# Four chunks of layer 1's attention values: from the context projection to the selective scan

## The reference

```
x = x + xattn0(layernorm(x), ctx, ctx)      # 16 heads of 32
x = x + scan(layernorm(x))                  # selective scan, 8 states, 256 inner channels
x = x + moe0(layernorm(x))
x = x + xattn1(layernorm(x), ctx, ctx)
x = x + delta_rule(layernorm(x))
x = x + moe1(layernorm(x))

def xattn(q, k, v):
    qp, kp, vp = q @ W_q + b_q, k @ W_k + b_k, v @ W_v + b_v
    out = softmax(qh @ kh.T / sqrt(32)) @ vh        # per head
    return out_of_heads @ W_o + b_o
```

## Time and profile before

| | us |
|---|---|
| median of 3 runs | 3893.53 |
| lowest, highest | 3889.25, 3896.72 |
| the profiled execution | 3890.58 |
| its span, first to last instruction | 3889.3 |
| projection, to attention's first matmul | 0 to 815.9 |
| attention of layer 0, to its last exchange | 815.9 to 1720 |
| scan stage | 1720 to 1825 |
| experts of layer 0, queries of layer 1 | 1825 to about 2165 |
| mean granted TensorE clock, share of full speed | 0.957 |

### The profile page before, as it was taken

One profiled execution on the slowest core, in us unless ns is written; L12 is line 12 of the kernel. 1 busy time (PEld: TensorE's weight loads), 2 busy tenths in 40 slices (PEclk: granted clock), 3 DMA queues, 4 the chain that ended last, 5 costly groups with the idle time before them and its releaser, 6 DMA issues. The chain is left out here.

```text
span 3889.3 us, 46028 instructions
## 1 busy us (share of the span) xinstructions
PE 3610.6 (93%) x17868; PEld 2320.1 (60%) x17868; DVE 2531.3 (65%) x3462; ACT 1920.3 (49%) x1962; POOL 1775.6 (46%) x744
## 2 busy tenths in 40 slices
PE   7999999989999999986797999999999886799997
PEld 6777778755555555432674545555554475688886
DVE  3222234357777777637796877777776465699997
ACT  2112311245555555542683455555556321577775
POOL 1112111159999999920000599999998320100000
PEclk9999999999999999996897899999999998899999
DMA  7555565543333333102686233333331101799996
GB/s 274 181 180 178 189 197 173 176 133 91 86 87 77 85 87 87 38 23 109 272 358 211 55 83 91 85 87 79 85 87 30 49 1 44 289 372 369 377 379 251
DMA packets 215944, 593.83 MB, mean 153 GB/s; under 512 B 42624, under 2 KB 108192, under 8 KB 161840
## 3 DMA queue, kind: packets, MB, share of 16 engines
q1 hardware_dynamic: 176944, 517.47, 40.9%
q10 hardware_dynamic: 36864, 67.13, 4.6%
q0 software_dynamic: 1920, 6.29, 0.5%
HBM read 470.64 MB, written 120.09 MB: 152 GB/s over the span
## 5 line engine op out<-in xcount | busy, mean ns | idle before, releaser
L642 DVE TENSOR_REDUCE maxima<-psum 128x1 f32<-128x512 f32 x2048 | 1290.8, 683 | 387.3 <-PE psum L637 383.7
L751 ACT ACTIVATE pt<-psum 128x1024 f32<-128x1024 f32 x1024 | 1018.7, 1025 | 703.1 <-PE psum L662 697.6
L765 POOL TENSOR_TENSOR exp_sums<-pt 128x1024 f32<-128x1024 f32 x342 | 818.5, 2394 | 266.4 <-PE psum L678 132.4
L637 PE MATMUL psum<-ks,first_q 96*128 96x512 f32 x2048 | 815.0, 447 | 22.0 <-DMA first_q<-q_parts 9.2
L768 POOL TENSOR_TENSOR exp_sums<-exp_sums,pt 128x1024 f32<-128x1024 f32 x310 | 737.0, 2377 | 45.7 <-ACT pt L751 1.4
L637 PEld LDWEIGHTS psum<-ks,first_q 96*128 96x128 f32 x2048 | 394.3, 193 | 480.9 <-DVE maxima L642 326.0
L674 PE MATMUL psum<-pt,vs 128*32 128x512 f32 x4096 | 675.8, 600 | 4.7 <-DVE head_rows L778 2.3
L678 PE MATMUL psum<-exp_sums,constants 128*32 128x512 f32 x1408 | 671.7, 600 | 0.0
L662 PE MATMUL psum<-qs,ks 97*128 97x512 f32 x2048 | 648.7, 400 | 15.1 <-ACT pt L751 15.1
L1428 DVE TENSOR_TENSOR moe_cut<-moe_raw,moe_cut 128x2048 fp32r<-128x2048 f32 x244 | 557.1, 2291 | 55.6 <-ACT moe_cut L1370 50.9
L1370 ACT CAST moe_cut<-moe_raw 128x2048 fp32r<-128x2048 f32 x244 | 467.1, 1921 | 64.7 <-PE psum L97 64.7
(11 more groups left out here) (310 smaller groups left out, 4401.3 us busy)
## 6 DMA issues: line engine op xcount, KB each, us to landing
moe_raw<-in_moe_w SPq DMA_DIRECT2D x244, 1024.0 KB, 7.8
ks<-k_parts SPq DMA_DIRECT2D x384, 256.0 KB, 4.7
k_parts<-kparts ACTq DMA_DIRECT2D x256, 256.0 KB, 3.0
cx<-in_ctx SPq DMA_DIRECT2D x32, 1024.0 KB
v_heads<-vrow SPq DMA_DIRECT2D x32, 1024.0 KB, 5.8
vs<-v_heads SPq DMA_DIRECT2D x32, 1024.0 KB, 5.3
first_q<-q_parts SPq DMA_DIRECT2D x96, 64.0 KB, 4.1
qs<-q_parts SPq DMA_DIRECT2D x96, 64.0 KB, 4.8
```

What stands on the lines that cost most here:

```text
L637: pe.matmul(self.c.bank[self.FIRST_BANK + k % 3], self.first_q[s][:, t * P:(t + 1) * P], self.ks[s][part][0:3 * DH, at:at + CHUNK], start= ...
L642: dve.tensor_reduce(self.maxima[:, h % 2, i % TT, i // TT:i // TT + 1], self.c.bank[self.FIRST_BANK + k % 3], X, ALU.max).then_inc(*self.f ...
L751: act.activation(self.pt[:, self.slot(h, b) + i:self.slot(h, b) + i + 2, :], self.c.psum[:, at:at + 2, :], ACT.Exp).then_inc(*self.exp.up())
L765: engine.tensor_tensor(to, self.pt[:, slot:slot + R, :], self.pt[:, slot + R:slot + 2 * R, :], ALU.add).then_inc(*signal.up())
```

## The change

Late chunks are n = 9, 11, 13 and 15 of layer 1, which are m = 25, 27, 29 and 31. Of these the projection makes keys only. The context chunks are the same for both layers, so SP stores both parts of each late chunk's context from `cparts` to `late_context` already in layer 0, in chunks 9, 11, 13 and 15 (four stores of 512 KB per chunk, in rows of 512 bytes out of SBUF), and in chunk 17 both parts of layer 1's value weights to `late_weights` (2 MB). The cast two chunks later (11, 13, 15, 17) also waits for the stores of the parts. In the scan stage a new class `LateValues` loads the weights (2 MB) and the context (16 tiles of 512 KB, room for four) and makes 16 units of 12 matmuls in banks 0 and 1: three (`FIRST_LATE`) before the first add, then one after each add. ScalarE copies unit i out of PSUM right behind the decay of step i, and SP stores each chunk's values.

The values' bias isn't added in the projection any more: VectorE copies value blocks there. In attention it loads `bv` (256 KB, broadcast) and adds its columns to each head's finished rows, in both layers; the last transposes wait for that add. The constants lose `pick` (1024 columns, 512 KB, not read by anything). The norm of the scan gives its memory back early, and the context tiles take its place: SP loads the first of them once the scan's first product is made.

```diff
@@ ProjectContext @@
+    LATE = (9, 11, 13, 15)
-            self.bv = c.sb(st, "bv", [P, 2, D], side="right")
+        def store_parts(m):
+            if m in self.LATE:
+                late = self.LATE.index(m)
+                sp.wait_ge(*self.ctx_low.at(m + 1))
+                for t in range(CHUNK // P):
+                    sp.dma_start(S["late_context"][...], self.cparts[:, m % 2, :, :, t * P:(t + 1) * P]...)
...
+            if m == NCHUNK + 1:
+                sp.wait_ge(*self.w_low.at(4))
+                for part in range(2):
+                    sp.dma_start(S["late_weights"][part]..., self.w["v"][part][:]...)
...
@@ on_pe, on_act, on_dve @@
+            if m - NCHUNK in self.LATE:
+                continue
...
-                dve.tensor_tensor(self.vrow[:, :, t, :], bank..., self.bv[:, l, :]..., ALU.add)
+                dve.tensor_copy(self.vrow[:, :, t, :], bank...)
...
@@ split_chunk on ScalarE @@
+            if m - 2 in self.LATE:
+                act.wait_ge(*self.parts_out.at((self.LATE.index(m - 2) + 1) * (CHUNK // P)))
@@ CrossAttention.finish_head on VectorE @@
+            rows = self.rows[:, :, h * DH:(h + 1) * DH]
+            dve.tensor_tensor(rows, folded[:, :, 0:DH], self.total..., ALU.mult).then_inc(*self.finished.up())
+            if h == 0:
+                dve.wait_ge(*self.wo_in.at(3))
+            dve.wait_ge(*self.finished.at(h + 1))
+            dve.tensor_tensor(rows, rows, self.bv[:, None, h * DH:(h + 1) * DH].to_broadcast([P, TT, DH]), ALU.add).then_inc(*self.biased.up())
@@ CrossAttention.on_pe, before the last transposes @@
-        pe.wait_ge(*self.finished.at(HEADS))
+        pe.wait_ge(*self.biased.at(HEADS))
@@ LateValues @@
+    def load_context(self, sp, u):
+        if u >= self.ROOM:
+            sp.wait_ge(*self.made.at(u - self.ROOM + 1))
+        sp.dma_start(self.context[:, u % self.ROOM]..., self.S["late_context"][...])
+    def on_pe(self, pe, u):
+        pe.wait_ge(*self.context_in[u % self.ROOM].at(u // self.ROOM + 1))
+        if u > 1:
+            pe.wait_ge(*self.copied.at(u - 1))
+        for k in range(KD):
+            last = product(pe, self.banks[u % 2], [self.context[...]], [self.w[...]], k == 0, k == KD - 1)
+        last.then_inc(*self.made.up())
+    def on_act(self, act, u):
+        act.wait_ge(*self.made.at(u + 1))
+        act.copy(self.rows[:, i % 2, :, t, :], self.banks[u % 2]...).then_inc(*self.copied.up())
@@ SelectiveScan @@
+        self.late.load_weights(sp)
+        sp.wait_ge(*self.h_made.at(KD))
+        for u in range(self.late.ROOM):
+            self.late.load_context(sp, u)
...
+        for u in range(self.FIRST_LATE):
+            self.late.on_pe(pe, u)
         for i in range(self.STEPS):
-            if i:
-                add(i - 1)
-        add(self.STEPS - 1)
+            add(i)
+            if self.FIRST_LATE + i < self.late.units:
+                self.late.on_pe(pe, self.FIRST_LATE + i)
...
         for i in range(self.STEPS):
             decays(i)
+            if i < self.late.units:
+                self.late.on_act(act, i)
```

More of the change, by code:

```diff
@@ L230, in on_pe @@
                 last.then_inc(*self.k_made.up())
-                beside(m * self.UNITS + b)
+                beside(self.unit(m) + b)
+            if m - NCHUNK in self.LATE:
+                continue
             if n == 0:
@@ L240, in on_pe @@
                 last.then_inc(*self.v_made.up())
-                beside(m * self.UNITS + KD + t)
+                beside(self.unit(m) + KD + t)
     def on_act(self, act):
@@ L293, in on_act @@
                 split_chunk(m + 1)
-            for t in range(CHUNK // P):
-                beside(m * self.UNITS + KD + t)
+            for t in range(CHUNK // P if m - NCHUNK not in self.LATE else 0):
+                beside(self.unit(m) + KD + t)
     def on_dve(self, dve):
@@ L327, in on_dve @@
                     split_weights(3)
-                beside(m * self.UNITS + b)
+                beside(self.unit(m) + b)
+            if m - NCHUNK in self.LATE:
+                continue
             if m:
-                dve.wait_ge(*self.v_out.at(m))
+                dve.wait_ge(*self.v_out.at(self.valued(m)))
             for t in range(CHUNK // P):
@@ L817 @@
     CB, TAPS, RING = INNER // P, 3, 3
+    FIRST_LATE = 3
     STEPS = DSTATE * CB
@@ L854, in run @@
             self.y_made, self.out_made, self.x_added = c.signals(st, "y_made scan_out_made scan_x_added")
+            with ExitStack() as place:
+                self.norm = Normalize(c, place, self.x, "ln_s")
+            self.late.hold_context(st)
             self.loads(c.sp)
@@ L858, in run @@
             self.on_pe(c.pe)
+            for s in self.late.out:
+                c.sp.wait_ge(*s.all())
             c.barrier()
@@ L872, in loads @@
             sp.dma_start(self.terms[:, which], self.S["bc"][which].rearrange("s n -> (s n)").partition_broadcast(P).rearrange("p (s n) -> p s n", s=DSTATE)).then_inc(*self.term_in[which].up())
+        for u in range(self.late.ROOM, self.late.units + self.late.TILES):
+            if u < self.late.units:
+                self.late.load_context(sp, u)
+            if u % self.late.TILES == self.late.TILES - 1:
+                self.late.store(sp, u // self.late.TILES - 1)
     def on_pe(self, pe):
@@ L1980, in constants @@
         "spare": (EXPERTS + j[:, :TT]) * P + i,
-        "pick": np.concatenate([(i == s) & (j >= 0) for s in range(DSTATE)], 1),
     }
```

92 lines of the change are left out of this document (67 added, 25 removed).

## The result

The changed kernel took 3904.8 us (median of 11 runs, 3898.0 to 3912.5), the kernel before 3892.0 (11 runs, 3887.6 to 3896.7): ratio 1.0035, 95% interval 1.0025 to 1.0044. By the ratio that is 13.6 us slower (9.7 to 17.1), by more than the 0.2% that a measurement can tell. The forecast was +1.6, a change that can't be measured. The time lies in the stated range, but above the forecast's own band (3887 to 3903), in the case "slower" that had 0.28.

The account below looks back on a forecast made before the run. TensorE bounds attention and seemingly the projection, where a second chain through ScalarE and GpSimd is almost as long. The terms 0.3 - 12.2 + 2 + 4 - 0.8 + 5.8 + 2 + 0.5 gave +1.6 us: 3895 us, range 3882 to 3911.

Parts of the forecast that it names:

- case "slower": Whole kernel: slower by over 0.2%, made up of rivals 2 to 4 and the forecast's upper edge; chance 0.28.
- opening: Projection's start: value biases and constants not loaded, 1 MB less among the loads; -0.8 us (0 to -1.5).
- heads: Attention: each bias add waits behind GpSimd, first scores come late; +2 us (0 to +8), and +0.5 at layer ends.
- saved parts: Chunks 9, 11, 13, 15: context stores compete with key stores, 0.5 us each; +2 us (0 to +20).
- weights: Chunk 17: 2 MB in long rows delays key stores, TensorE lacks parts; +4 us (+1 to +6).
- scan: Scan stage: ScalarE's copy ahead of the decay lengthens steps, +4.7 us; second decay waits, +1.1; together +5.8 (+4.6 to +7).
- late chunks: Chunks 25 to 30: chain covers removed work, late chunks 22.8 us, restarts 1.4 us each; +0.3 us (-5 to +5).
- chunk 31: Projection's last chunk: no next chunk, so the next stage's first matmul comes earlier; -12.2 us (-11 to -13).
- rival 2: Saved chunks: parts hold up key stores as in chunk 21, 5.7 us each, 3916 us; half of it, 3905; chance 0.16.
- 1: Projection: key stores give way, late chunks take 21.5 us, saving parts is free; 3882 us; chance 0.14.
- 3: Scan: matmuls run at half clock, +52 us instead of 5.8, 3941 us; chance 0.04.
- 4: Attention: TensorE pays each head's wait in full, 52 us, 3945 us; chance 0.03.

Follow-up runs that it names:

- e9: The changed kernel with no values left out of the projection, so those of four chunks are made twice, there and in the scan; 3919.0 us, ratio 1.0067.
- e3: The changed kernel with ScalarE's cast of the next chunk's context moved from behind the fourth key block's stores to behind the second's; 3877.8 us, ratio 0.9968.
- e5: The changed kernel with all values made in the projection, no units in the scan and no weights stored, context parts still saved; 3907.1 us, ratio 1.0035.
- e1: The changed kernel with all values made in the projection, nothing saved, no units in the scan; smaller opening loads and heads' bias stay; 3892.4 us, ratio 1.0006.
- e8: e5 with each saved chunk stored by two transfers in 8 KB rows instead of four in 512-byte pieces; 3916.8 us, ratio 1.0064.
- e6: e3 with ScalarE also making the decay of step i+1 ahead of the copy of unit i; 3868.4 us, ratio 0.9939.
- e12: The changed kernel with only ScalarE's decay of step i+1 put ahead of the copy of unit i; 3897.4 us, ratio 1.0011.
- e10: e1 with the values' bias added twice at each head; 3908.9 us, ratio 1.0034.
- e4: The kernel before with the same early cast as e3 and nothing else; 3888.4 us, ratio 0.9994.
- e11: The changed kernel with the early cast, the decay ahead of the copy, and the weights stored in chunk 25 instead of 17; 3868.2 us, ratio 0.9932.

## Why the prediction was right or wrong

| step | predicted | measured (time) | in the profiles |
|---|---|---|---|
| opening, heads, layer ends | +1.7 | +2.3 +/- 3.5 | +0.8 projection, -1.6 and -0.4 attention |
| saved parts and weights | +6 | +12.1 +/- 6.4 | +7.2 chunks 9 to 16, +4.6 chunk 17 |
| scan | +5.8 | +11.7 +/- 7.4 | +5.3 loop, +2.8 behind it |
| late chunks and chunk 31 | -11.9 | -12.5 +/- 6.3 | -9.0 (e9) to -10.2 (before) |

**The sum: in the range, but not for its reasons.** The forecast was no measurable change, and the time moved by 13.6 us, 12 more. By the sum the projection would end 6.7 us earlier (the prediction's last paragraph says some 8); it ended 1.9 later. The step that failed is the price of the saved parts, below. That 3904.8 lies inside 3882 to 3911 is due to the room left for rival 2, not to that rival's mechanism, and that "half of it, 3905" is the measured number is luck.

**Late chunks: right, cause shown.** From the first key block of chunk 25 to that of chunk 31 it is 146.0 us instead of 143.3, +2.7 for the +0.3 forecast; TensorE idle for 10 us in each late chunk and restarting at 0.50, as said. The late chunks, from start to start on TensorE, take 22.5, 23.1 and 22.8 us, the forecast's 22.8. What was low is the restart: from TensorE's start to the first key block it is 4.95 us in chunk 26 instead of 3.00, so 2.0 for the 1.4 taken. (The rows it was read from give 1.5, since 3.13 less 1.63 is that.) That the chain behind the fourth key block covers the removed work was shown by shortening it (e3). Chunk 31 gave 12.7, for the 12.2.

**Saved parts: the mis-sized term.** The step was "I take 0.5 us each, near the first, since small rows let other stores pass sooner". It measured 1.8 each by profile, 7.3 for the four, and e5 - e1 is 11.3 +/- 6.4. That small pieces hold the key stores less than long rows is right (e8). What it left out is that ScalarE's own issues get longer while SP issues the pieces (1.4 to 1.7 us a pair instead of 0.81), which is more of the delay than the third block's wait, and that the chunk behind a saved one, bound by TensorE, can't give the delay back. Rival 2's full price of 5.7 a chunk, read from chunk 21, is near that of long rows: 6.1 in e8. **Weights:** +4 taken, 4.6 to 5.9 in chunk 17 of the profiles.

**Scan: mechanism right, parts of the size wrong.** The chain through ScalarE's copy was named as the limit, and e6 and e12 show it. The steps it holds measured 3.82 us in twelve steps, for the 3.74 in thirteen of the forecast: +5.3 for its +4.7. The +1.1 for the second decay isn't seen, the first two steps take 3.38. The two errors partly cancel. What the sum lacked is the stage's end: the prediction looked at TensorE's clock while units run, not at what the clock does when they stop, +2.8 us in three of four profiles with units in this order.

**The heads: right, but near an edge.** The add takes 1.69 us in the median, and 1.63 to 1.74 in 28 of the 32 heads, as forecast from neg_max (which has one tensor as its input, so that it was a stand-in for the add), and the Trainium skill's rule (SBUF — State Buffer, "Who interferes with whom"), that a VectorE instruction with two SBUF inputs contends with a GpSimd instruction that reads SBUF, agrees with it: 1693 ns in the median, 292 where GpSimd is free. It costs TensorE nothing that can be seen (+2 was taken); the first scores of the next block, named as what would come late, do so one add later (e10).

**Opening.** At chunk 9 the changed kernel is 2.6 us ahead and e1 4.3, more than the 0.8; but e1 has lost it by chunk 31 (782.8 against 782.0). An early lead is not kept where later chunks scatter by as much, so the term was worth about nothing at the projection's end.

**Rivals.** 1 is out: a late chunk's third key block is still held for 4.33 us, and comes 11 us after the chunk's start, not under 10. 2 is out by its own sign, "from 2 us per chunk on", in the profiles (1.8), and no key block of chunks 9 to 15 waits over 8 us for stores; in time e5 - e1 is 2.8 +/- 1.6 a chunk and can't exclude half its price. 3 is out: the clock is 1.00 in the loop. 4 is out: e1 is 2.3 us above before, not 52.

**Open.** The two profiles differ by 13.5 us: +1.9 in the projection, -2.6 attention 0, +2.6 up to the first scan, +5.3 scans, -0.5 behind them, +2.3 experts and queries, +1.5 attention 1, +3.0 after it. The 2.6 and 2.3 are scatter (the same two stretches are 56.9 and 300.1 us in e4, which has nothing of the change, 54.6 and 302.9 in before). After attention 1 it is 822.9 us in before and 823.1 in e4, and 824.6 to 830.1 in the twelve kernels that have the heads' bias. The trace places this: from attention 1's last output row to ScalarE's last table load it is 280.5 and 280.8 us in before and e4, and 282.2 to 287.7 in the twelve; behind that load all fourteen take 541.6 to 542.8. In the first stretch TensorE is granted half clock for 88.7 us in before and e4, and for 92.2 to 109.2 us in the twelve, and over the fourteen profiles the length of the stretch goes with it (correlation 0.96: 280.5 us at 88.7, 283.5 at 92.2 in the changed kernel, 287.7 at 109.2 in e6 and e11). So these 3 us go with the granted clock, in instructions that no edit touches. Whether the heads' bias brings it about isn't shown: no run was aimed at it, and before and e4 are two executions.

## What to carry to other kernels

Work taken off the busiest engine is worth only what the next chain leaves: measure that chain per step, with its instructions' order in each queue, before moving anything. Where it is almost as long, first shorten it, here by one cast moved two key blocks up, and then the move pays (26 us instead of 10 in the late chunks; the whole change then gains 10 us instead of costing 14). A bulk store or a copy is priced by the small urgent things behind it: put the decay ahead of the copy, and look at whether the next step, not only this one, has room to give a delay back.

## What was unexpected of the hardware

Parts saved in 8 KB rows delay another queue's 256 KB key stores more than the same bytes in 512-byte pieces: the third key block of chunk 15 waited 9.77 us against 5.47, and a saved chunk cost 6.1 us against 1.8, although SP's issues took 1.9 us instead of some 11. The small pieces cost elsewhere: a pair of ScalarE's issues beside them took 1.66 us instead of 0.81.

A 0.29 us instruction on an engine with a quarter of its time free cost 0.43 us per head (e10), where a 1.7 us one before it had cost nothing that can be seen: free time on average says nothing of the moment.

TensorE's granted clock fell from 1.00 to 0.50 at the end of the scan stage in e9, after a loop in which it was busy almost throughout, when gaps of 0.8 us had come between adds; in the changed kernel's profile, with the same gaps, it stayed at 1.00.
